# L2 feed-forward: the input scale moved from the first matrix into the turned activations

## What is computed

```python
W1 = (2 * w1_bits - 1).astype(x.dtype)
W3 = (2 * w3_bits - 1).astype(x.dtype)
h = jnp.einsum('bsi,mi->bsm', x * scaling0, W1)
h = h * scaling2
out = jnp.einsum('bsm,om->bso', h, W3)
out = out * scaling4 + bias
```

## Time and profile before

| what | us |
|---|---|
| median of 3 runs | 4204.03 |
| lowest and highest | 4203.64 and 4207.63 |
| profiled execution | 4209.37 |
| its span in the trace | 4207.6 |
| busy PE / DVE / ACT / POOL | 3712.3 / 2792.1 / 2269.8 / 1909.4 |
| steps 3 to 26 of the list, from the trace | about 3473 to 3618 |

### The profile page before, as it was taken

The page is one execution under the profiler, slowest core; times in us unless marked ns, Lnnn a source line. Parts: engine busy times, 40 slices in busy tenths (PEclk is TensorE's granted clock), DMA queues, the critical chain, the costliest instruction groups (busy, mean ns, idle before and its releaser), DMA issues.

```text
span 4207.6 us, 62985 instructions
## 1 busy us (share of the span) xinstructions
PE 3712.3 (88%) x21602; PEld 1850.4 (44%) x21602; DVE 2792.1 (66%) x4493; ACT 2269.8 (54%) x3911; POOL 1909.4 (45%) x1578
## 2 busy tenths in 40 slices
PE   3889998889888779999999999999999975867899
PEld 2344443223322345555555555555555542443344
DVE  4444345664675468888888888988888866566322
ACT  4533224455455466667666666766676644453222
POOL 4600000000000348787777878777777774463000
PEclk9999987899888899999999999999999997898999
DMA  3200011001100100000000000000000010012000
GB/s 104 63 6 1 1 31 16 1 2 26 27 7 4 40 12 1 25 13 25 13 20 18 4 25 10 25 13 20 18 7 24 1 49 15 23 46 76 29 10 20
DMA packets 62919, 91.62 MB, mean 22 GB/s; under 512 B 12406, under 2 KB 36489, under 8 KB 62597
## 3 DMA queue, kind: packets, MB, share of 16 engines
q1 hardware_dynamic: 61928, 86.94, 7.2%
q10 hardware_dynamic: 672, 0.59, 0.1%
HBM read 73.85 MB, written 6.85 MB: 19 GB/s over the span
## 4 chain that ended last, share of the span: by engine, by line
PE 62%; DVE 14%; issue 8%; ACT 6%; POOL 3%; DMA 1%; DVEq 0%; ACTq 0%; POOLq 0%; SPq 0%
PE psum L329 13%; PE psum L331 13%; PE psum L330 13%; PE psum L1563 3%; DVE arena L1725 3%; PE psum L1536 2%; PE psum L2670 2%; PE psum L2658 2%; PE psum L2666 2%; PE psum L2627 2%; PE psum L1547 2%; DVE x L2352 1%; PE psum L2649 1%; PE psum L1532 1%; ACT xn L218 1%
## 5 line engine op out<-in xcount | busy, mean ns | idle before, releaser
L329 PE MATMUL psum<-xt_hi,arena 128*128 128x512 f16 (+2 forms) x2272 | 875.0, 385 | 31.1 <-DVE arena L588 9.1
L330 PE MATMUL psum<-xt_lo,arena 128*128 128x512 f16 (+2 forms) x2272 | 873.4, 384 | 0.0
L331 PE MATMUL psum<-xt_hi,arena 128*128 128x512 f16 (+2 forms) x2272 | 872.9, 384 | 0.0
L2453 POOL TENSOR_TENSOR arena<-arena 128x1024 f16<-128x1024 f16 x256 | 515.4, 2033 | 49.5 <-DVE arena L2264 32.3
L329 PE MATMUL psum<-arena 128*128 128x512 f16 (+1 forms) x1152 | 421.8, 370 | 61.2 <-DVE arena L3081 19.6
L1725 DVE TENSOR_REDUCE arena<-psum 128x1 f32<-128x512 f32 (+3 forms) x608 | 366.4, 655 | 162.8 <-PE psum L1536 161.8
L1676 ACT ACTIVATE arena<-psum 128x512 f32<-128x512 f32 x576 | 320.1, 598 | 285.0 <-PE psum L1547 187.4
L331 PE MATMUL psum<-arena 128*128 128x512 f16 (+1 forms) x1152 | 421.9, 370 | 0.0
L330 PE MATMUL psum<-arena 128*128 128x512 f16 (+1 forms) x1152 | 421.9, 370 | 0.0
L1481 POOL TENSOR_TENSOR rs<-sd,epsc 128x1 f32<-128x1 f32 x15 | 8.1, 540 | 830.0 <-DVE sd L1773 830.0
L329 PEld LDWEIGHTS psum<-xt_hi,arena 128*128 128x128 f16 (+1 forms) x2272 | 224.8, 99 | 279.8 <-issue 17.3
(11 more groups left out here) (354 smaller groups left out, 7532.5 us busy)
## 6 DMA issues: line engine op xcount, KB each, us to landing
arena<-m_wi SPq DMA_DIRECT2D x64, 320.0 KB, 2.9
arena<-m_wo SPq DMA_DIRECT2D x32, 256.0 KB, 2.6
arena<-arena SPq DMA_DIRECT2D x90, 64.0 KB, 2.6
x<-L_attn_x SPq DMA_DIRECT2D x4, 1024.0 KB, 5.2
out<-x SPq DMA_DIRECT2D x4, 1024.0 KB, 4.4
arena<-gate_wT SPq DMA_DIRECT2D x16, 224.0 KB, 2.5
arena<-up_wT SPq DMA_DIRECT2D x16, 224.0 KB, 2.5
arena<-down_wT SPq DMA_DIRECT2D x14, 256.0 KB, 2.6
```

The source lines that it names most:

```text
L329: nc.tensor.matmul(out, lh, rh, start=start, stop=False)
L330: nc.tensor.matmul(out, lh, rl, start=False, stop=False)
L331: return nc.tensor.matmul(out, ll, rh, start=False, stop=stop)
L2453: nc.gpsimd.tensor_tensor(m4_ar[:, q], heads[q].broadcast_to([P, HG, P]), m4_le.unsqueeze(1).broadcast_to([P, HG, P]), ALU.mult).then_inc( ...
```

## The change

The first matrix keeps only its exact plane, `+-WS` (a power of two), and the input scale goes into the two planes of the turned activations. `hi` for tiles 0 to 15 becomes four instructions, one for each channel part, because the scale is one value a partition and differs from part to part. `lo` becomes four in the same way. The seven tiny instructions of `parts` and the low plane of the matrix are gone. `hidden` makes two products where `three` made three. ACT and DVE wait for the six transfers of the scales, matrices and biases (`s5_in` at 96) at the first `hi` and `lo`; before, DVE waited for them at `parts`.

```diff
-        s5_c = carve(80464, [6, KT], F32)
-        s5_ch = carve(80464 + 96, [KT], F16)
-        s5_w1h = carve(88656, [KT, C], F16)
-        s5_w1l = carve(92752, [KT, C], F16)
+        s5_w1 = carve(88656, [KT, C], F16)
...
-                    nc.scalar.activation(xt_hi[:, :, (u % NT) * P:(u % NT + 1) * P],
-                                         psum[:, x_bank(u), :].rearrange("p (k c) -> p k c", k=KT),
-                                         ACT.Copy).then_inc(xt_h, 1)
+                    tok = slice((u % NT) * P, (u % NT + 1) * P)
+                    if u < NT:
+                        if u == 0:
+                            act.wait_ge(s5_in, 96)
+                        for k in range(KT):
+                            v = nc.scalar.activation(xt_hi[:, k, tok], psum[:, x_bank(u), k * P:(k + 1) * P], ACT.Copy,
+                                                     scale=s5_s0[:, k:k + 1])
...
+            if u < NT:
+                if u == 0:
+                    dve.wait_ge(s5_in, 96)
+                for k in range(KT):
+                    v = nc.vector.scalar_tensor_tensor(out=xt_lo[:, k, tok], in0=psum[:, x_bank(u), k * P:(k + 1) * P],
+                                                       scalar=s5_s0[:, k:k + 1], in1=xt_hi[:, k, tok], op0=ALU.mult,
+                                                       op1=ALU.subtract)
...
-                    nc.vector.tensor_scalar(s5_w1h[:, k, :], s5_raw[:, 0, k, :], s5_c[:, 2, k:k + 1], s5_c[:, 3, k:k + 1],
-                                            ALU.mult, ALU.add)
-                    nc.vector.tensor_scalar(s5_w1l[:, k, :], s5_raw[:, 0, k, :], s5_c[:, 4, k:k + 1], s5_c[:, 5, k:k + 1],
-                                            ALU.mult, ALU.add).then_inc(s5_w, 1)
+                    nc.vector.tensor_scalar(s5_w1[:, k, :], s5_raw[:, 0, k, :], 2.0 * WS, -WS, ALU.mult,
+                                            ALU.add).then_inc(s5_w, 1)
...
-                        last = three(pe, psum[:, f % 2, :], s5_w1h[:, k, fc], s5_w1l[:, k, fc],
-                                     xt_hi[:, k, g * GW:(g + 1) * GW], xt_lo[:, k, g * GW:(g + 1) * GW], k == 0, k == KT - 1)
+                        nc.tensor.matmul(psum[:, f % 2, :], s5_w1[:, k, fc], xt_hi[:, k, g * GW:(g + 1) * GW],
+                                         start=(k == 0), stop=False)
+                        last = nc.tensor.matmul(psum[:, f % 2, :], s5_w1[:, k, fc], xt_lo[:, k, g * GW:(g + 1) * GW],
+                                                start=False, stop=(k == KT - 1))
```

More of the change, by code:

```diff
@@ L2895, in act_late @@
                     act.wait_ge(x_tr, n + 1)
-                    nc.scalar.activation(xt_hi[:, :, (u % NT) * P:(u % NT + 1) * P],
-                                         psum[:, x_bank(u), :].rearrange("p (k c) -> p k c", k=KT),
-                                         ACT.Copy).then_inc(xt_h, 1)
+                    tok = slice((u % NT) * P, (u % NT + 1) * P)
[5 more added lines that the diff above has]
+                                                     scale=s5_s0[:, k:k + 1])
+                    else:
+                        v = nc.scalar.activation(xt_hi[:, :, tok], psum[:, x_bank(u), :].rearrange("p (k c) -> p k c", k=KT),
+                                                 ACT.Copy)
+                    v.then_inc(xt_h, 1)
                 elif what == "w6":
@@ L2959, in low_plane @@
             dve.wait_ge(xt_h, u + X5 + 1)
-            nc.vector.tensor_tensor(xt_lo[:, :, tok], psum[:, x_bank(u), :].rearrange("p (k c) -> p k c", k=KT),
-                                    xt_hi[:, :, tok], ALU.subtract).then_inc(xt_ok, 1)
+            if u < NT:
[5 more added lines that the diff above has]
+                                                       op1=ALU.subtract)
+            else:
+                v = nc.vector.tensor_tensor(xt_lo[:, :, tok], psum[:, x_bank(u), :].rearrange("p (k c) -> p k c", k=KT),
+                                            xt_hi[:, :, tok], ALU.subtract)
+            v.then_inc(xt_ok, 1)
         def dve_late(dve, ch):
@@ L3020, in dve_late @@
                 elif what in ("parts", "planes"):
+                    k = u
                     if what == "parts":
                         dve.wait_ge(s5_in, 96)
[L3023 to L3031, removed]
-                    nc.vector.tensor_scalar(s5_w1h[:, k, :], s5_raw[:, 0, k, :], s5_c[:, 2, k:k + 1], s5_c[:, 3, k:k + 1],
-                                            ALU.mult, ALU.add)
-                    nc.vector.tensor_scalar(s5_w1l[:, k, :], s5_raw[:, 0, k, :], s5_c[:, 4, k:k + 1], s5_c[:, 5, k:k + 1],
-                                            ALU.mult, ALU.add).then_inc(s5_w, 1)
+                    nc.vector.tensor_scalar(s5_w1[:, k, :], s5_raw[:, 0, k, :], 2.0 * WS, -WS, ALU.mult,
+                                            ALU.add).then_inc(s5_w, 1)
                 elif what == "w3":
```

## The result

| | us |
|---|---|
| before, median of 20 runs | 4202.94 (4193.33 to 4209.26) |
| after, median of 20 runs | 4208.82 (4198.98 to 4219.85) |
| ratio after to before | 1.0016, 95% interval 1.0009 to 1.0024 |
| forecast | 4207.3, or +3.3 |

The account below looks back on a forecast made before the run. PE looked busiest, but the changed stretch was taken as bound by a serial loop, then ACT and DVE, then PE in steps 24 to 26. Step terms summed to +3.3 on the 4204.0 median, giving 4207.3 us, range 4201 to 4215.7.

Parts of the forecast that it names:

- Three regimes: Steps 3 to 6 a serial loop, 7 to 17 and 19 to 23 set by ACT and DVE, 24 to 26 by PE.
- Four small instructions: Splitting hi and lo in four: hi 1.13 us (+0.53), lo 1.04 us (+0.44), against 0.60 each before.
- Planes and `parts`: Steps 3 to 6: one matrix plane 0.33 us for two at 0.91 (-0.58), parts gone (-1.23); with additions, +0.3 in all.
- The wait for the transfers: At the first hi, a new wait for six transfers, put at 0 to 0.3 us and taken as 0.
- Step 7: Four fewer PE matmuls shorten ACT's 1.54 us wait, of which hi and lo use 0.97: -0.6 us, -0.2 with step 8.
- Steps 9 to 12: Only lo adds to the path, hi stays hidden behind statistics: +1.6 us for these four steps in the table.
- Step 17: No hidden here; lo and most of hi show on the path: +0.8 us.
- rival 1: The clock: longer PE waits start bursts at 1.2 GHz, costing +5.6 us from step 16 on, so 4212.9; chance 0.12.
- Steps 24 to 26: PE is the path; fewer matmuls save between 0 and 1.72 us, taken as -1.1, at 6.6 us a step in 24 and 25.
- 2 (no overlap of small instructions): Whole stretch: lo costs +0.84 and hi +0.78, 8.4 us more than forecast, so 4215.7; chance 0.07.
- 3 (PE is the bound): Whole stretch: all 64 matmuls come off the path, 13.8 us faster, so 4190.2; chance 0.04.
- 4 (additions hidden): Whole stretch: the extra instructions cost nothing and only the savings show, so 4198.2; chance 0.03.

Follow-up runs that it names:

- e8_lo1: Changed kernel with lo as one unscaled instruction again, hi still in four; y_norm of step 2 to y_norm of step 26 took 141.84 us, 5.9 under after.
- e6_two: Kernel before with the third product of each hidden left out; y_norm of step 2 to y_norm of step 26 took 141.11 us, ratio 0.9996.
- e3_split: Kernel before with hi and lo each in four scaled instructions, nothing else changed; median 4216.04 against 4204.47 us, ratio 1.0028.
- e2_unscaled: Changed kernel without the input scale, hi and lo one instruction each as before; median 4201.68 against 4204.47 us, ratio 0.9998.
- e1_third: Changed kernel with a third matmul put back into each hidden product; y_norm of step 2 to step 26 took 150.30 us, ratio to before 1.0019.

## Why the prediction was right

The time, 4208.8, lies in the range and on the side that was forecast, and the class (within 0.2%) is the one that had 0.77. The size was low by 2.6 in the medians of the first set, and by 0.2 in the two traces that are compared step by step. That closeness is in part luck: against the second trace of before the same stretch measured +4.7, and inside it misses of -0.4, +0.5 and +0.35 (steps 9, 17 and 22) stand beside smaller ones of the other sign. The prediction also held that anything under 0.2% can't be told from none. With twenty runs of each, 0.16% was told from none, and the interval reaches 0.24%.

- **The bound.** Three regimes and what is on the path in each: borne out by `e8_lo1` (`lo` in all sixteen steps), `e6_two` (PE in four places only) and the rows after. Steps 8, 10 and 11 came out at 5.83 and 5.84 (5.85 forecast), PE's own steps 24 and 25 at 6.54 and 6.48 (6.6 forecast), and no `h_hi` of steps 7 and 13 waited for PE.
- **Four small instructions.** 1.13 and 1.04 forecast, 1.14 and 1.04 found. The step that mattered was to take the fixed price from the distance between starts (0.13 for the same kind at 512 columns) and not from the duration; four durations would have been 1.47 and 1.37. The copies alone were longer than I put them, 0.358 to 0.377 against 0.34 to 0.35, which the sum of four hides. "VectorE: DVE Perf Modes" of the Trainium skill, with its 512 elements or more, was right that the split costs, though its section speaks of instructions that read SBUF, and `hi` reads PSUM. The estimates from its table, 0.375 and 0.43, were a little under the 0.43 and 0.54 found, which include the scale operand. They would have made the sum 1.8 lower (16 x 0.065 + 8 x 0.10), not 1.6.
- **Planes and `parts`.** 0.33 a plane and steps 3 to 6 at +0.34 against +0.3. The wait for the transfers cost nothing: ACT's idle time before the first `hi` was 1.22 and ended by PE, as before.
- **Step 7.** -0.32 with step 8, as forecast, but on this trace only. The idle time that the term was read from is the clock's: 1.54 in one execution and 0.72 in the other. In the second the 0.97 of `hi` and `lo` is more than the wait, so the term would have been +0.25. It should have had the range +0.25 to -0.6.
- **Steps 9 to 12.** +1.25 against +1.6. Before had a wait of 0.42 between two tiny DVE instructions in step 9, where 0.05 is usual; after has it in step 22. Neither was in the forecast, and they cancel.
- **Step 17.** +1.35 against +0.8. Of the difference 0.45 is one set of transposes at half clock. That is the price rival 1 named for such a set, but not its mechanism: `e3_split`, with all the `hidden` work, had the same set at half clock, and `e2_unscaled`, with a third of it gone, had not. Why the clock rose later stays open. The rival's 4 us at half rate is near what the trace of before has behind pauses, 3.4 us from 3513.12 on and 5.2 us from 3531.73 on. The rest of that rival did not come: steps 19 to 25 stayed at 6.00 but for the 0.35 of step 22, with PE idle up to 2.24 us.
- **Steps 24 to 26.** -1.23 with step 24's -0.18, against -1.1.
- **Rivals.** 2 (no overlap of small instructions) is out by the rows, 3 (PE is the bound) by `e6_two` and `e1_third`, 4 (additions hidden) by `e3_split`. In steps 19 to 24 the granted clock was 1.00.

## What to carry to other kernels

Look for the engine that is waited for in the stretch, not the one that is busiest: 13.8 us of TensorE work bought 1.9 to 3.1 us, the weight work that fell away 3.6 (1.82 in step 3 and 0.58 in each of steps 4 to 6 of `e2_unscaled`), and the small instructions that took their place cost 10.1 to 11.3. The three need not add up, because two savings can use up one wait. Price a small instruction by the distance between starts of the same kind, less its columns. And where a stage is a serial loop of three engines, overlapping its pieces through a second PSUM bank and giving the waiting engine a piece of the work is worth a try: it gave 0.94 us a step in three steps and 2.5 to 3.7 us in the stretch, at least as much as the 64 matmuls, and it leaves the products as they are.

## What the runs showed of the hardware

- The granted clock after a pause is not set by the length of the pause alone: transposes took 1.07 us after 2.29 us of idle PE and 0.66 after 2.23. The prediction said of the first row that it agrees with its rule of idle gaps; the second does not. After the change they took 1.11 after only 1.31 in step 16; there PE had been at half clock before the pause already (all eight `y` matmuls took 0.63 or 0.64). In step 22, at full clock before, they took 0.66 after 2.24:

```profile
3593.11 0.66 PE L3105 MATMUL psum<-ident,xn 128*128 128x128 f32 x4 [2.24 <-ACT xn L218]
```

- The same program got the full clock sooner in one execution than in another, so a wait for PE behind a pause is not a constant: 1.54 and 0.72 us in two executions of before.
- DVE has a pause of about 0.36 us (0.42 where 0.05 is usual) whose place depends on the program and repeats between executions. In the changed kernel, instructions in order of time in step 22:

```profile
3589.18 0.16 DVE L2998 BATCH_NORM_AGGREGATE mv<-st 128x2 f32<-128x6 f32 x1
3589.75 0.18 DVE L3002 BATCH_NORM_AGGREGATE mv<-st 128x2 f32<-128x6 f32 x1 [0.42 <-DVE mv L2998]
```

  It stands in the same step in both traces of each kernel (9 before, 22 after), and at neither place in `e3_split`. `e6_two` has it in step 9 and `e1_third` in step 22. What it is stays open; no run here was made for it.
- A scale read from SBUF costs ACT 0.09 us an instruction (0.367 against 0.273 for 128 columns out of PSUM), and DVE about 0.06 (0.75 against 0.69 for 512 columns, in an instruction of another kind).
